# Exponent factors of a Mamba-2 layer by way of DRAM: three loads a chunk in place of sixteen copies, and new orders on every engine

## What is computed

```python
xn = layernorm(x)
z, xBC, dt = split(xn @ W_in)                  # 512 | 768 | 8 columns
dt  = softplus(dt + dt_bias)
xBC = silu(causal_conv4(xBC));  X, B, C = split(xBC)   # 8 heads of 64 | 128 | 128
cum = cumsum(dt * -exp(A_log)) within a chunk of tokens
L   = exp(cum[s] - cum[t]) for t <= s, else 0          # per head
Y   = (C B^T * L) (X dt)  +  C state * exp(cum)        # in the chunk + from the state
y   = rmsnorm((Y + X * D) * silu(z)) * rms_w @ W_out
out = x + layernorm(xn + y) * ln_g + ln_b  +  tanh(xn @ F1 @ F2 @ F3 + bias)
```

## Time and profile before

| | |
|---|---|
| three runs | 805.11, 805.52, 807.39 us, median 805.52 |
| profiled execution | 806.79 us, of which the span of the trace is 805.1 us |
| PE busy | 736.7 us, 92% |
| PE weight load busy | 600.2 us, 75% |
| DVE busy | 635.3 us, 79% |
| ACT busy | 580.9 us, 72% |
| POOL busy | 640.8 us, 80% |
| mean granted PE clock | 0.968 |
| instructions | 17418 |
| DMA | 38.53 MB, mean 48 GB/s |

### The profile page before, as it was taken

One profiled execution on the slowest core, in us unless ns is written; L12 is line 12 of the kernel. 1 busy time (PEld: TensorE's weight loads), 2 busy tenths in 40 slices (PEclk: granted clock), 3 DMA queues, 4 the chain that ended last, 5 costly groups with the idle time before them and its releaser, 6 DMA issues.

```text
span 805.1 us, 17418 instructions
## 1 busy us (share of the span) xinstructions
PE 736.7 (92%) x4856; PEld 600.2 (75%) x4856; DVE 635.3 (79%) x1257; ACT 580.9 (72%) x1427; POOL 640.8 (80%) x996
## 2 busy tenths in 40 slices
PE   7988989998999989999998999999899998999974
PEld 5767767787878778777777777777777777877754
DVE  2888778896969779697786978779697887959754
ACT  3895859877677877778677776867778686777751
POOL 2557868997888979798797988878798897878854
PEclk7999999999999999999999999999999999999987
DMA  6002021202112111111202112120211211011120
GB/s 204 3 22 62 18 79 30 65 19 69 34 37 67 37 57 33 52 45 44 67 18 68 42 31 65 44 69 17 66 40 33 67 43 41 29 36 35 31 66 28
DMA packets 60079, 38.53 MB, mean 48 GB/s; under 512 B 7120, under 2 KB 59472, under 8 KB 59984
## 3 DMA queue, kind: packets, MB, share of 16 engines
q1 hardware_dynamic: 58768, 37.40, 15.1%
q10 hardware_dynamic: 1216, 0.02, 0.1%
HBM read 27.70 MB, written 8.65 MB: 45 GB/s over the span
## 4 chain that ended last, share of the span: by engine, by line
SPq 41%; PE 37%; issue 13%; DVE 3%; ACT 2%; DMA 2%; POOL 1%; ACTq 0%; DVEq 0%; POOLq 0%
SPq L311 17%; SPq L312 17%; PE ring L2626 15%; SPq L326 5%; PE yd_bank L2786 5%; PE bg_bank L2626 4%; PE xt_bank L2757 2%; PE e_bank L2742 2%; PE xt_bank L2769 2%; PE xt_bank L2712 1%; PE bg_bank L2798 1%; DVE ring L1166 1%; DMA lay<-in_f_dram 1%; SPq L281 1%; PE bg_bank L2797 1%
## 5 line engine op out<-in xcount | busy, mean ns | idle before, releaser
L2626 PE MATMUL ring<-xhl,wh 128*128 128x512 f32 x620 | 213.8, 426 | 0.0
L1179 DVE SCALAR_TENSOR_TENSOR xs<-ring,cw,xs 128x512 f32<-128x512 f32 x273 | 195.6, 737 | 7.1 <-ACT xs L2087 5.1
L2626 PEld LDWEIGHTS ring<-xhl,wh 128*128 128x128 f32 x620 | 110.5, 190 | 34.7 <-issue 18.0
L2626 PE MATMUL ring<-xhl,wl 128*128 128x512 f32 x310 | 122.7, 396 | 0.0
L634 POOL TENSOR_TENSOR lay<-lay,xd 128x512 f32<-128x512 f32 x62 | 79.4, 1281 | 47.9 <-DVE lay L1217 47.7
L2157 ACT ACTIVATE xdt<-xt_bank,dts 128x64 f32<-128x64 f32 x512 | 112.0, 343 | 6.5 <-PE xt_bank L2712 6.3
L2087 ACT ACTIVATE xs<-ring,cb,cw 128x512 f32<-128x512 f32 x91 | 71.3, 784 | 52.5 <-PE ring L2626 52.4
L2137 ACT ACTIVATE e_bank<-e_bank 128x512 f32<-128x512 f32 x128 | 75.7, 594 | 32.8 <-PE e_bank L2742 32.5
L1217 DVE TENSOR_TENSOR lay<-xt_bank,grow 128x512 f32<-128x512 f32 x62 | 42.7, 688 | 64.9 <-issue 53.8
L1208 DVE SCALAR_TENSOR_TENSOR lay<-e_bank,btg 128x512 f32<-128x512 f32 x128 | 86.9, 682 | 0.2 <-ACT e_bank L2137 0.2
L2626 PE MATMUL bg_bank<-woh,yts 128*128 128x256 f32 x252 | 77.5, 308 | 6.1 <-DVE ss L1251 3.4
(11 more groups left out here) (186 smaller groups left out, 1914.8 us busy)
## 6 DMA issues: line engine op xcount, KB each, us to landing
grow<-scratch SPq DMA_DIRECT2D x124, 128.0 KB, 2.9
xin<-in_x_dram SPq DMA_DIRECT2D x32, 256.0 KB, 2.7
out_dram<-res SPq DMA_DIRECT2D x31, 256.0 KB, 2.7
right<-rows SPq DMA_DIRECT2D x256, 2.0 KB
left<-rows SPq DMA_DIRECT2D x256, 2.0 KB
lay<-in_w_in_dram SPq DMA_DIRECT2D x1, 776.0 KB, 7.0
lay<-in_w_in_dram SPq DMA_DIRECT2D x1, 512.0 KB, 9.4
sq<-in_w_out_dram SPq DMA_DIRECT2D x1, 512.0 KB, 5.9
```

Of the source, the lines that this page charges most:

```text
L1179: v.scalar_tensor_tensor(out=to, in0=conv_bank(j, ct), scalar=cw[:, ct, t:t + 1], in1=to, op0=ALU.mult, op1=ALU.add).then_inc(tap_done[ct], 1)
L2626: last = mul(out, a, c, start=first and i == 0, stop=i == n - 1)
```

## The change

The rows take the way over DRAM, and the factor matrices hold them without zeros between them: slot i of `right` has its rows at partitions 0 to 7 for every i, and `left` at partitions 32 to 39. The tables beside them, the matmul and its shape are the same.

```diff
+        factors = nc.dram_tensor("factors", (BUF, C, 2, Q * H, P), F32, kind="Internal").ap()
...
-            def put_growth(j, b):
+            def put_rows(j, b):
                 sp.wait_ge(sums_read, j + 1)
+                apart(sp)
+                sp.wait_ge(rows_done, j + 1)
                 apart(sp)
                 if begun(j - BUF):
                     for q in range(Q):
                         sp.wait_ge(grow_loaded[q], 32 * (C * (j - 1) - 1))
                         apart(sp)
-                sp.dma_start(scratch[b], growth[:, :]).then_inc(growth_put, 16)
+                    for c in range(C):
+                        sp.wait_ge(factors_in[c], 48 * (j - 1))
+                        apart(sp)
+                for c in range(C):
+                    sp.dma_start(factors[b, c].rearrange("l n t -> n l t"), rows[c * Q * H:(c + 1) * Q * H, b].bitcast(F32)).then_inc(rows_put, 16)
+                sp.dma_start(scratch[b], growth[:, :]).then_inc(rows_put, 16)
...
             def spread_factors(j, b, c):
                 k = C * j + c
-                sp.wait_ge(rows_done, j + 1)
+                sp.wait_ge(rows_put, 48 * (j + 1))
...
-                for i in range(FOUR):
-                    for low in range(2):
-                        at, n = c * Q * H, 2 * FOUR * i + FOUR * low
-                        sp.dma_start(right[n:n + FOUR, c, i].bitcast(F32), rows[at + i:at + Q * H:FOUR, b, low].bitcast(F32)).then_inc(factors_in[c], 16)
-                        sp.dma_start(left[LO + n:LO + n + FOUR, c, i].bitcast(F32),
-                                     rows[at + FOUR * i:at + FOUR * (i + 1), b, low].bitcast(F32))\
-                            .then_inc(factors_in[c], 16)
+                sp.dma_start(right[0:2 * FOUR, c].bitcast(F32), factors[b, c].rearrange("l (g i) t -> (l g) i t", i=FOUR))\
+                    .then_inc(factors_in[c], 16)
+                for low in range(2):
+                    at = LO + FOUR * low
+                    sp.dma_start(left[at:at + FOUR, c].bitcast(F32), factors[b, c, low].rearrange("(g i) t -> i g t", i=FOUR))\
+                        .then_inc(factors_in[c], 16)
...
-                sp.wait_ge(growth_put, 16 * (j + 1))
+                sp.wait_ge(rows_put, 48 * (j + 1))
```

SP's loop body becomes:

```diff
             def one_pass(j, b, b1):
-                load_again(j + 1, b1, 1)
                 spread_growth(j - 1, b1, 0, 0)
+                spread_growth(j - 1, b1, 0, 1)
+                store(j - 2, b, 0)
+                spread_growth(j - 1, b1, 1, 0)
                 spread_factors(j - 1, b1, 1)
-                spread_growth(j - 1, b1, 0, 1)
-                spread_growth(j - 1, b1, 1, 0)
-                store(j - 2, b, 0)
                 load_again(j + 2, b, 0)
                 store(j - 2, b, 1)
-                put_growth(j, b)
                 spread_growth(j - 1, b1, 1, 1)
+                put_rows(j, b)
+                load_again(j + 2, b, 1)
                 spread_factors(j, b, 0)
```

More of the change, by code:

```diff
@@ L1404, in one_pass @@
                 low_part(j, b, 1)
+                weigh(j - 1, b1, 0, 1, 1)
+                scale_off(j - 1, b1, 0, 1)
+                y_low(j - 1, b1, 0, 0)
+                add_bias(j, b, 0)
                 weigh(j - 1, b1, 0, 1, 0)
-                scale_off(j - 1, b1, 0, 1)
-                add_bias(j, b, 0)
-                y_low(j - 1, b1, 0, 0)
-                weigh(j - 1, b1, 0, 1, 1)
+                tap(j, b, 2, 0)
             def head():
@@ new lines, in tail @@
+                join_spill(12, 0, 1)
+                apply_gate(11, 1, 1, 0)
+                last_h(11, 1, 0, 0)
+                tap(12, 0, 1, 2)
+                new_state(11, 1, 1, 0)
+                tap(12, 0, 4, 2)
+                y_low(11, 1, 1, 0)
+                low_rows(12, 0)
+                join_spill(12, 0, 0)
+                tap(12, 0, 5, 0)
+                weigh(11, 1, 1, 1, 0)
+                tap(12, 0, 5, 1)
+                scale_off(11, 1, 1, 1)
+                tap(12, 0, 5, 2)
@@ new lines, in tail @@
+                join_spill(13, 1, 1)
+                apply_gate(12, 0, 1, 0)
+                last_h(12, 0, 0, 0)
+                tap(13, 1, 1, 2)
+                new_state(12, 0, 1, 0)
+                tap(13, 1, 4, 2)
+                y_low(12, 0, 1, 0)
+                low_rows(13, 1)
+                join_spill(13, 1, 0)
+                tap(13, 1, 5, 0)
+                weigh(12, 0, 1, 1, 0)
+                tap(13, 1, 5, 1)
+                scale_off(12, 0, 1, 1)
+                tap(13, 1, 5, 2)
@@ new lines, in tail @@
+                join_spill(14, 0, 1)
+                apply_gate(13, 1, 1, 0)
+                last_h(13, 1, 0, 0)
+                tap(14, 0, 1, 2)
+                new_state(13, 1, 1, 0)
+                tap(14, 0, 4, 2)
+                y_low(13, 1, 1, 0)
+                low_rows(14, 0)
+                join_spill(14, 0, 0)
+                tap(14, 0, 5, 0)
+                weigh(13, 1, 1, 1, 0)
+                tap(14, 0, 5, 1)
+                scale_off(13, 1, 1, 1)
+                tap(14, 0, 5, 2)
@@ new lines, in tail @@
+                join_spill(15, 1, 1)
+                apply_gate(14, 0, 1, 0)
+                last_h(14, 0, 0, 0)
+                tap(15, 1, 1, 2)
+                new_state(14, 0, 1, 0)
+                tap(15, 1, 4, 2)
+                y_low(14, 0, 1, 0)
+                low_rows(15, 1)
+                join_spill(15, 1, 0)
+                tap(15, 1, 5, 0)
+                weigh(14, 0, 1, 1, 0)
+                tap(15, 1, 5, 1)
+                scale_off(14, 0, 1, 1)
+                tap(15, 1, 5, 2)
@@ L2841, in one_pass @@
             def one_pass(j, b, b1):
+                conv_project(j - 1, b1, 2)
+                x_tokens(j - 2, b, 1, 0)
+                branch_project(j - 1, b1, 1, 1)
+                branch_project(j - 1, b1, 1, 0)
+                y_diag(j - 2, b, 0, 1)
+                states(j - 2, b, 0, 1)
+                exponents(j - 2, b, 1, 0, 1)
+                conv_project(j - 1, b1, 3)
+                exponents(j - 2, b, 1, 0, 0)
+                y_off(j - 2, b, 1, 0)
+                square_sum(j - 2, b, 0, 0)
+                conv_project(j - 1, b1, 1)
+                conv_project(j - 1, b1, 4)
+                conv_project(j - 1, b1, 0)
+                exponents(j - 2, b, 1, 1, 1)
+                exponents(j - 2, b, 1, 1, 0)
+                x_tokens(j - 2, b, 1, 1)
+                square_sum(j - 2, b, 0, 1)
+                y_diag(j - 2, b, 1, 0)
+                out_project(j - 2, b, 0, 0)
+                states(j - 2, b, 1, 0)
+                conv_project(j - 1, b1, 5)
+                sums(j - 1, b1)
+                z_project(j - 1, b1, 0)
                 y_off(j - 2, b, 1, 1)
                 z_project(j - 1, b1, 1)
+                out_project(j - 2, b, 0, 1)
                 x_tokens(j - 1, b1, 0, 0)
-                out_project(j - 2, b, 0, 1)
                 y_diag(j - 2, b, 1, 1)
@@ L2974, in head @@
                 out_project(0, 0, 1, 1)
+                exponents(1, 1, 0, 1, 0)
                 y_diag(1, 1, 0, 0)
```

1713 lines of the change are left out of this document (816 added, 897 removed).

## The result

The changed kernel takes 752.07 us in the median of four runs (751.01 to 752.86); the kernel before took 805.32 us beside it (803.94 to 807.39). The ratio is 0.9336, with an interval of 0.9312 to 0.9359.

What follows compares the result with a forecast made beforehand. SP's issuing from `sums` on was taken as the slow link that sets each step. Gains of 31.4 us (steady part), 4 (start) and 2 (end), together 37.4, off 806.8 gave 769 us, range 759 to 790.

Steps and rivals of the forecast that it cites:

- What bounds the kernel: Each step's end depends on SP's issuing from `sums` on; PE's three largest waits, 36.1 us together, lie in that chain.
- the clock hangs on the same chain: PE's granted clock drops behind a late `scale_off`, to 0.66 for 4 us in one instance.
- Issues removed and added: SP's list, per step: 20.1 us of copies leave, about 5 us of puts and loads come; issuing falls from 28 to 13.
- The round trip: Rows to DRAM and factors back, before the first exponents: factors there at 464.2, wanted about 467.3, margin some 3 us.
- the wait for `residual_bias`: SP's `load_again` ahead of the factors waits for POOL until 460.9, bringing the factors to 465.1, still 2.2 us early.
- C: Rival: the trip over DRAM is the new late wait, PE standing 2.3 us before the first exponents: 800 us, chance 0.05.
- D: Rival: SP stuck behind `load_again`, PE standing 3.5 us a step: slower, 815 us, chance 0.04.
- B: Rival: another wait takes over, costing PE 1.3 us more a step, a step of 46.6 us: 788 us, chance 0.20.
- Growth: SP's growth loads of chunk 0 in place by 470, wanted about 482.4; DVE's 2.96 us and PE's 1.00 and 0.78 go.
- The step: Steady step falls from 47.77 to 45.3 us, 0.9 above PE's floor; over 12.7 steps 31.4 us.
- The start and the end: Earlier first growth and late `x_tokens` at both ends: 4 us gained at the start, 2 at the end.
- Orders: New lists of PE, DVE, ACT and POOL do the same work; PE's floor of a step is 44.4 us.

Runs made afterwards that it cites:

- experiment 1: The kernel before with only the factors' way over DRAM, all lists in their old orders but for one put in step 3: 764.33 us, ratio 0.9494.
- experiment 11: experiment 1 with the growth loads of chunk 1, sequence 1, moved ahead of `put_rows` in SP's list: 742.09 us, ratio 0.9239.
- Experiment 3: The kernel before, copies kept, with the growth of chunk 0, sequence 1, issued ahead of the 16 copies of chunk 1: 786.52 us, ratio 0.9772.
- experiment 8: The changed kernel with 8 or 16 extra 8 KB loads a chunk ahead of the factor loads: 753.57 us with 8, 810.55 us with 16.
- experiment 4: experiment 1 with SP's loop and tail from the changed kernel, the other four engines keeping their old lists: 743.60 us, ratio 0.9234.
- Experiment 9: The changed kernel with two pairs of neighbours swapped, one in PE's list and one in DVE's: 752.22 us, ratio 0.9332.
- experiments 6 and 7: 6: experiment 4 with PE's `states` and `conv_project` 5 ahead of `sums`, 787.49 us; 7: changed kernel with PE's old list from step 4 on, 914.42 us.

## Why the prediction was wrong in size

The runs split the 53 us like this. The last column goes by the ratios, since each kernel was measured beside the kernel before, and that took 803.8 to 805.3 us:

| kernel | us | ratio | us against the one above |
|---|---|---|---|
| before | 805.3 | 1 | |
| factors by way of DRAM, old orders (1) | 764.3 | 0.9494 | -41 |
| growth (1, 1) ahead of `put_rows` (11) | 742.1 | 0.9239 | -21 |
| the changed kernel, with all new orders | 752.1 | 0.9336 | +8 |

**What bounds the kernel: right.** The chain from `sums` over SP's copies to the growth, `scale_off`, `x_tokens` and `branch_project` was the one that set the step. Experiment 3 shows it for the late growth (19 us) and experiment 1 for copies and growth together (41 us), and SP's queue went from 41% of the chain to no place in it. That the clock hangs on the same chain held, too: 0.968 became 0.988.

**Issues removed and added: right in sign, the price of the loads too high.** I took 0.63 us for each new load and 1.5 us for the three puts. The puts were priced right: they are issued from 473.24 to 474.70. The `left` loads and the factor puts of the changed kernel (duration min/median/max in ns):

```profile
L320 SPq DMA_DIRECT2D left<-factors x64: 255/288/548, 38.0 to 710.6; - x64
L302 SPq DMA_DIRECT2D factors<-rows x32: 313/374/429, 35.2 to 696.1; - x32
```

The loads, those of `right` (282 ns) too, are issued in 0.28 to 0.29 us, half of what I took from the copies. With the growth, stores and loads of a step, SP issues for about 10 us, where I said 13. What was wrong is the choice of row: the pitch of a copy from SBUF to SBUF stood for a load from DRAM. It cost the sum nothing, since SP is not what bounds the new kernel.

**The round trip: right in its course, the landing too dear.** From the start of `sums` I had 6.6 us to the last factor load's issue, and 7.5 with the wait for `residual_bias`; it was 6.2. I had 2.2 us for its landing; it was 1.6 (experiment 8). The puts land after 1.5 us in the median, where I had 1.4:

```profile
DMA to landing us min/median/max: 1.4/1.5/2.9
```

I said that the first exponents would be wanted 11.9 us after the start of `sums` (467.3 against 455.42); they run at 11.8. The margin was 3.7 us where I had 2.2 with the wait for `residual_bias`. That this wait ends last in SP's list, 6.5 us after `a_all`, was right (a load goes out at 475.77, 0.10 after the POOL operation ends at 475.67, which is 6.3 after the end of `a_all`). The Trainium skill, "DMA: Bandwidth & Descriptors", section "Latency and other measured facts", gives the latency of HBM as 2 us at high load against 0.2 on average; by an estimate from that page two such legs would have cost 11 us. No wait of PE for a factor is in this trace, at a DMA share of 0.17 in the steady part: the measured landings decide, 1.5 and 1.6 us for the whole of each leg. Whether the page's average holds inside them is shown by no run here. The rivals C (800 us) and D (815 us) are excluded by the same lines, and B (788 us) since no wait of PE comes back in every step.

**Growth: right for chunk 0, overlooked for chunk 1.** I followed the growth of chunk 0 through SP's new list and found it early enough, as it is. That `spread_growth(1, 1)` now stands ahead of `put_growth`'s successor is in the list of the change, and I gave it no price. It is worth some 21 us on the old orders (experiment 11) and, with all of SP's list, 68 us on the new ones (820.5 against 752.1). It is no gain over the kernel before, where this growth was in time for PE (461.12, experiment 1). It keeps the new path from making it late. That could be read from the list: behind the wait for ACT's `growth` stood a load whose data had long been there, and the change puts the wait for the rows and two more puts in front of it. The length of SP's wait (166.2 us) does not tell it, since it is 164.8 us in the changed kernel. My sum did not show this, because it went by the floor of a step and not by what each edit gives.

**The step: 45.3 us was the term that failed.** I took the floor of 44.4 and left 0.9 us of waits in each step, by analogy with the gaps that SP did not cause before. The measured step is 44.52, with 0.34 us of idle PE in the step shown. POOL at 90% (40.15 of 44.49 us) costs PE no wait that comes back. With my own factor, 12.7 x (47.81 - 44.52) = 41.8 us, 10 more than the 31.4 of the sum. Even my low end for a step, 44.7, was too careful: an early step of 44.27 stood in the earlier trace rows, and experiment 4 does the same work in 43.79. The gaps at full clock for which I found no cause in SP's list went together with the others. They were SP's as well: in experiment 11, with the old lists of the four engines, PE is idle for 1.3 us in all eleven steps.

**The start and the end: too small.** I took 4 and 2 us. The start, up to step 1, gave 2.1. Steps 1 to 3 gave 10.8 and the end 5.7, but my 12.7 steady steps reach 1.7 steps into these stretches (1.7 x 3.29 = 5.6 us). So what I had called start and end was worth 2.1 + 10.8 + 5.7 - 5.6 = 13 us rather than 6. I had counted one late `x_tokens` in each. Up to step 1 PE's idle time did not fall at all; the gain is busy time, at a clock of 0.88 and 0.91. Of the 10.8 us of steps 1 to 3, 7.3 are idle time of PE and 3.5 busy time (clock 0.98 and 1.00), of the 5.7 us at the end 3.2 and 2.5 (0.90 and 0.93). So the waits there were more than the one that I had read, and the clock gave back the rest.

The two terms that were mis-sized, the step by 10.4 us and start and end by 7, make up the 17 us of the miss.

**Orders: not neutral.** I costed the new orders of four engines at nothing, beyond waits that stay. They lose 8.5 us against experiment 4, and they make the path necessary: with the copies they give 865 us. This error goes the other way than the two terms above and hides part of them: against experiment 4, which has not got this loss, 769 is 25 us too high and not 17. The mechanism by which a step at full clock with almost no wait of PE takes 44.5 in one order and 43.8 us in the other stays open. Of the 8.1 us in eleven steps 5.5 are busy time of PE (485.92 against 480.39) and 2.5 idle time; the number of matmuls and the granted clock are the same. Experiment 9 removed two waits of weight loads and found 0.2 us; experiments 6 and 7 put larger waits in their place and show nothing about it. A place for `load_again` behind the factors was not tried in the changed kernel by itself.

## What to carry to other kernels

Read a list that is run strictly in order for what stands behind each wait, whatever the queue's total load: here a transfer whose data had been ready for a step stood behind the puts, and one line moved gave some 21 us, half as much as the whole new path. A change that adds work to such a list makes late what stood behind it and was just in time. When a chain that stalls every engine is removed, cost the new step by the best step that the trace has shown (44.27 here), not by that plus the gaps of the slower steps, and count the clock that PE gets back at the start and the end, too. Lists that were ordered together are one piece: a single engine's list from another set cost up to 162 us, so test the path with the old orders before new ones are searched, since the old ones were the better here.

## What the runs showed of the hardware

- The time that SP takes to issue a DMA does not go by its size. In the kernel before a copy of 2 KB from SBUF to SBUF took 577 ns in the median; in the changed one a load of 8 KB from DRAM took 288 ns, a put of 16 KB 374 ns and a growth load of 128 KB, repeated over 64 partitions, 608 ns.

```profile
L312 SPq DMA_DIRECT2D left<-rows x256: 577/577/677, 38.3 to 766.7; - x128
```

- Two DMAs in a row, one into DRAM (1.5 us to landing) and one out of it (1.6), were shorter than sixteen issues of 0.63 us each with one landing: 6.2 against 13.0 us from `sums` to the last issue.
- A wait costs more than its length. Behind 4.74 us without work PE's clock was granted at 0.50 for 4 us, behind 2.08 us at 0.75, and the kernels in which such a wait came in every step had a mean clock of 0.924 and 0.948. Against the changed kernel their PE was idle for 70.4 and 30.3 us more and busy for 43.3 and 29.5 us more, with the same matmuls. In experiment 1, with a wait of 1.0 to 1.7 us in each step, the mean clock was 0.986.
